# Retention and mixture-of-experts layer: down projections of three groups as three rounded products, centred first pairs, new orders

## The reference

```python
x = x + attn(layernorm(x))
x = x + ffn(layernorm(x))

# attn: 4 heads, q and k of 32, v of 64; q, k get rotary embeddings
scores = einsum('bhtd,bhsd->bhts', q, k) * decay_mask      # gamma_h ** (t - s) for t >= s, else 0
o = einsum('bhts,bhsd->bhtd', scores, v)
o_n = o * rsqrt(mean(o * o, -1) + EPS) * g_norm_w
attn = (o_n * silu(x @ Wg.T)) @ Wo.T

# ffn: 8 experts of which each token takes 2, and a shared expert; all 128 -> 128 -> 128
comb = softmax(x @ gate_w.T), top 2 kept and scaled to sum 1, the others 0
y = sum_e comb[:, e] * (silu(x @ up_w[e] + up_b[e]) @ down_w[e] + down_b[e])
ffn = y + silu(x @ sh_up_w + sh_up_b) @ sh_down_w + sh_down_b
```

## Time and profile before

| | |
|---|---|
| Median of 3 runs (lowest, highest) | 142.51 us (142.03, 142.53) |
| The profiled execution | 142.45 us, of which the span is 140.7 us |
| Busy: PE, PEld, DVE, ACT, POOL | 93%, 74%, 74%, 56%, 35% of the span |
| Mean granted TensorE clock | 0.988 of 2.4 GHz |
| Moved by DMA | 12.50 MB |

### The profile page before, as it was taken

The page is one execution under the profiler, slowest core; times in us unless marked ns, Lnnn a source line. Parts: engine busy times, 40 slices in busy tenths (PEclk is TensorE's granted clock), DMA queues, the critical chain, the costliest instruction groups (busy, mean ns, idle before and its releaser), DMA issues.

```text
span 140.7 us, 3363 instructions
## 1 busy us (share of the span) xinstructions
PE 130.8 (93%) x1249; PEld 103.7 (74%) x1249; DVE 104.2 (74%) x311; ACT 78.6 (56%) x138; POOL 48.8 (35%) x69
## 2 busy tenths in 40 slices
PE   5659899899999999999998999999999999999990
PEld 5549799798978988886885675776557655589990
DVE  3589999989689997998796949679443982113983
ACT  4223937955562478555659762697745864471130
POOL 5458897937372342815222804502000000000000
PEclk9977999999999999999999999999999999999999
DMA  4999910000000000097000097010197200002002
GB/s 113 296 274 317 334 68 0 5 0 5 0 5 0 2 5 0 17 320 270 2 5 0 16 317 270 2 56 19 47 276 283 75 2 0 0 0 79 0 0 75
DMA packets 8659, 12.50 MB, mean 89 GB/s; under 512 B 1298, under 2 KB 5676, under 8 KB 8644
## 3 DMA queue, kind: packets, MB, share of 16 engines
q1 hardware_dynamic: 8356, 12.10, 26.7%
q10 hardware_dynamic: 288, 0.20, 0.4%
HBM read 11.20 MB, written 1.10 MB: 87 GB/s over the span
## 4 chain that ended last, share of the span: by engine, by line
PE 72%; DVE 10%; DMA 5%; SPq 4%; ACT 3%; issue 3%; DVEq 0%
PE bY L1238 17%; PE bU L1061 8%; PE bU L1062 7%; PE bU L1063 7%; DMA UW<-upw 5%; PE bA L1135 5%; PE bA L1211 4%; PE bU L1154 3%; PE bA L1129 3%; PE bA L1105 2%; PE bM L1154 2%; PE bU L1145 2%; PE bM L1180 1%; DVE SC L724 1%; SPq L267 1%
## 5 line engine op out<-in xcount | busy, mean ns | idle before, releaser
L497 ACT ACTIVATE HB<-bU,UB 128x512 f32<-128x512 f32 x36 | 24.3, 686 | 22.0 <-PE bU L1063 21.7
L1238 PE MATMUL bY<-HG,DW 128*128 128x512 f32 x48 | 24.5, 594 | 0.0
L848 DVE TENSOR_TENSOR HG<-CB,HB 128x512 f32<-128x512 f32 x24 | 16.3, 688 | 10.9 <-ACT HB L497 10.2
L353 POOL TENSOR_TENSOR RR<-SS,NHALF 128x8 f32<-128x8 f32 x8 | 13.5, 1684 | 25.9 <-DVE SS L743 25.9
L1061 PE MATMUL bU<-XH,UWH 128*128 128x512 f32 x36 | 21.5, 597 | 0.0
L1062 PE MATMUL bU<-XL,UWH 128*128 128x512 f32 x36 | 14.2, 395 | 0.0
L1063 PE MATMUL bU<-XH,UWL 128*128 128x512 f32 x36 | 14.2, 393 | 0.0
L1061 PEld LDWEIGHTS bU<-XH,UWH 128*128 128x128 f32 x36 | 6.8, 189 | 5.5 <-issue 4.3
L1238 PEld LDWEIGHTS bY<-HG,DW 128*128 128x128 f32 x48 | 8.4, 190 | 2.5 <-issue 1.4
L724 DVE TENSOR_TENSOR SC<-bA,MASK 128x512 f32<-128x512 f32 x16 | 10.2, 679 | 0.0
L1062 PEld LDWEIGHTS bU<-XL,UWH 128*128 128x128 f32 x36 | 6.8, 190 | 3.4 <-issue 3.4
(11 more groups left out here) (180 smaller groups left out, 317.8 us busy)
## 6 DMA issues: line engine op xcount, KB each, us to landing
CB<-scratch SPq DMA_DIRECT2D x12, 512.0 KB, 5.8
ROT<-rotary_tables SPq DMA_DIRECT2D x8, 256.0 KB, 4.5
out<-OUT SPq DMA_DIRECT2D x8, 128.0 KB, 1.8
X<-x SPq DMA_DIRECT2D x7, 128.0 KB, 6.1
UW<-upw SPq DMA_DIRECT2D x1, 576.0 KB, 6.6
DW<-dnw SPq DMA_DIRECT2D x1, 576.0 KB, 5.5
W<-wqkvg SPq DMA_DIRECT2D x1, 256.0 KB, 3.7
W<-wqkvg ACTq DMA_DIRECT2D x1, 128.0 KB, 3.9
```

The lines of the kernel that those rows point to most:

```text
L353: pool.tensor_tensor(RR[:, n], SS[:, n], NHALF[:, 0:2 * H], ALU.pow).then_inc(rr.sem, 1)
L497: act.activation(HB[:, k, :], bU[(g * (E + 1) + k) % 2][:, :], ACT.Silu, bias=UB[:, e:e + 1]).then_inc(hid.sem, 1)
L848: dve.tensor_tensor(HG[:, k % RING, :], CB[:, k - 1, :], HB[:, k, :], ALU.mult).then_inc(gated.sem, 1)
L1238: pe.matmul(bY[:, :], DW[:, e * P:(e + 1) * P], HB[:, 0, :] if k == 0 else HG[:, k % RING, :], start=(k == 0), stop=(k == E)).then_inc(dow ...
```

## The change

Five things are done at once.

1. `down_proj` of groups 0 to 2 becomes a `product` of three matmuls. The weights DW are split once (`split_down` on ScalarE, `low_down` on GpSimd). The gated hidden values are split for each expert: `hi(g, k)` on ScalarE copies to HGH with rounding, `lo(g, k)` subtracts, on VectorE for k = 1, 4, 7 and on GpSimd for the others. HGH and HGL have RING = 3 buffers each. HG itself has 2, so `gating(g, k)` waits for the remainder of k - 2.
2. The first two pairs are centred only (`center1` in place of `normalize1`), so their normalization doesn't wait for the standard deviation. The factor RS1 is applied after the projections: as `scale` of ScalarE's `values` and `gates`, and in `rotary` and `rotate`. Pairs (1, 0) and (1, 1) are normalized on ScalarE, no longer on VectorE.
3. The rotations of pairs (0, 0) to (1, 1) and `low_w(1)` move from GpSimd to VectorE.
4. W's larger part is loaded from ScalarE's queue, behind its smaller part. On SyncE's queue CN falls behind X(3).
5. The orders of all engines and PLACE are laid out anew. XN1 and XN2 hold one group only, SLOTS goes from 4 to 3, TABLES from 6 to 5; the normalizations wait for the transposes of the group before.

```diff
-RING = 4
-SLOTS = 4
-TABLES = 6
-NORM1, NORM2 = 4, 4
+RING = 3
+SLOTS = 3
+TABLES = 5
+LO_V = (1, 4, 7)
+LO_P = (0, 2, 3, 5, 6, 8)
+NORM1, NORM2 = 2, 4
+FOLD = 2
...
+        DWH = sb("DWH", [P, (E + 1) * P], F32R)
+        DWL = sb("DWL", [P, (E + 1) * P], F32R)
...
-        HG = sb("HG", [P, RING, GC])
+        HG = sb("HG", [P, 2, GC])
+        HGH = sb("HGH", [P, RING, GC], F32R)
+        HGL = sb("HGL", [P, RING, GC], F32R)
...
+        def exact(k):
+            return HB[:, 0, :] if k == 0 else HG[:, k % 2, :]
+        def wait_low(eng, g, k):
+            if k in LO_V:
+                eng.wait_ge(g_lo_v.sem, g_lo_v.at(g, LO_V.index(k)))
+            else:
+                eng.wait_ge(g_lo_p.sem, g_lo_p.at(g, LO_P.index(k)))
...
             load_first_x(sp, 0)
-            sp.dma_start(W[:, QK:], wqkvg[:, QK:]).then_inc(ld_w[1].sem, 16)
             load_x(sp, 1)
...
+            def lo(g, k):
+                pool.wait_ge(g_hi.sem, g_hi.at(g, k))
+                pool.tensor_tensor(HGL[:, k % RING, :], exact(k), HGH[:, k % RING, :].bitcast(F32), ALU.subtract).then_inc(g_lo_p.sem, 1)
+            def low_down():
+                pool.wait_ge(dw_hi.sem, 1)
+                pool.tensor_tensor(DWL[:, :], DW[:, :], DWH[:, :].bitcast(F32), ALU.subtract).then_inc(dw_lo.sem, 1)
...
             act.dma_start(W[:, 0:QK], wqkvg[:, 0:QK]).then_inc(ld_w[0].sem, 16)
+            act.dma_start(W[:, QK:], wqkvg[:, QK:]).then_inc(ld_w[1].sem, 16)
...
+            def split_down():
+                act.wait_ge(ld_dn.sem, 16)
+                act.copy(DWH[:, :], DW[:, :]).then_inc(dw_hi.sem, 1)
+            def hi(g, k):
+                if k == 0:
+                    act.wait_ge(hid.sem, hid.at(g, 0))
+                else:
+                    act.wait_ge(gated.sem, gated.at(g, k - 1))
+                if k >= RING:
+                    act.wait_ge(down.sem, down.at(g, k - RING))
+                elif g:
+                    act.wait_ge(down.sem, down.at(g - 1, k + E + 1 - RING))
+                act.copy(HGH[:, k % RING, :], exact(k)).then_inc(g_hi.sem, 1)
...
+            def center1(g, p):
+                dve.wait_ge(mv1.sem, mv1.at(g, p))
+                for b in range(2):
+                    t = g * TILES + 2 * p + b
+                    last = dve.tensor_scalar(XN1[:, p, b * P:(b + 1) * P], X[:, t * P:(t + 1) * P],
+                                             MV1[:, t, 0:1], None, ALU.subtract)
+                last.then_inc(xn1.sem, 1)
...
+                if pair(g, p) < FOLD:
+                    dve.wait_ge(rs1.sem, rs1.at(g, p))
+                    for b in range(2):
+                        t = 2 * pair(g, p) + b
+                        dve.scalar_tensor_tensor(out=RA[:, p, b], in0=src[:, b * QK:(b + 1) * QK], scalar=RS1[:, t:t + 1], in1=cos,
+                                                 op0=ALU.mult, op1=ALU.mult)
...
-                if k > RING:
-                    dve.wait_ge(down.sem, down.at(g, k - RING))
+                if k > 2:
+                    wait_low(dve, g, k - 2)
                 elif g:
-                    dve.wait_ge(down.sem, down.at(g - 1, k + E - RING))
-                dve.tensor_tensor(HG[:, k % RING, :], CB[:, k - 1, :], HB[:, k, :], ALU.mult).then_inc(gated.sem, 1)
+                    wait_low(dve, g - 1, k + E - 2)
+                dve.tensor_tensor(HG[:, k % 2, :], CB[:, k - 1, :], HB[:, k, :], ALU.mult).then_inc(gated.sem, 1)
...
-                pe.matmul(bY[:, :], DW[:, e * P:(e + 1) * P], HB[:, 0, :] if k == 0 else HG[:, k % RING, :], start=(k == 0),
-                          stop=(k == E)).then_inc(down.sem, 1)
+                w = slice(e * P, (e + 1) * P)
+                product(bY[:, :], (DWH[:, w], DWL[:, w]), (HGH[:, k % RING, :], HGL[:, k % RING, :]), k == 0,
+                        k == E).then_inc(down.sem, 1)
...
-            keep_busy(10)
+            keep_busy(7)
             x1_t(0, 0)
+            keep_busy(2)
             x1_t(0, 1)
+            after(xl1, 0, 0)
             proj_qk(0, 0)
             proj_g(0, 0)
             after(xl1, 0, 1)
+            proj_g(0, 1)
             proj_qk(0, 1)
```

More of the change, by code:

```diff
@@ L393, in _ @@
             rstd1(0, 1)
-            low_w(1)
             rstd1(1, 0)
@@ new lines, in _ @@
+            hidden(1, 7)
+            hi(1, 5)
+            hidden(1, 8)
+            hi(1, 6)
+            hidden(2, 0)
+            hi(1, 7)
+            hidden(2, 1)
+            hi(1, 8)
+            hi(2, 0)
+            transposed_out(3, 1)
+            hi(2, 1)
+            hidden(2, 2)
+            sums(1)
+            hi(2, 2)
+            x2_norm(3, 0)
+            hidden(2, 3)
+            hidden(2, 4)
+            x2_hi(3, 0)
+            hi(2, 3)
+            x2_norm(3, 1)
+            hidden(2, 5)
@@ L715, in rotate @@
                 dve.wait_ge(rparts.sem, rparts.at(g, p))
+                if pair(g, p) < FOLD:
+                    for b in range(2):
+                        t = 2 * pair(g, p) + b
+                        last = dve.scalar_tensor_tensor(out=QKR[:, slot(g, p), b], in0=RB[:, p, b], scalar=RS1[:, t:t + 1],
+                                                        in1=RA[:, p, b], op0=ALU.mult, op1=ALU.add)
+                    last.then_inc(rot.sem, 1)
+                    return
                 dve.tensor_tensor(QKR[:, slot(g, p)].rearrange("r b n -> r (b n)"), RA[:, p].rearrange("r b n -> r (b n)"),
@@ new lines, in _ @@
+            proj_qk(2, 1)
+            after(rparts, 2, 0)
+            proj_v(2, 0)
+            proj_out(0, 0)
+            attend(1, 0)
+            after(x1, 0, 0)
+            out_t(0, 1)
+            after(rparts, 2, 1)
+            qk_t(2, 0)
+            after(v_sb, 2, 0)
+            qk_t(2, 1)
+            after(ogt, 0, 1)
+            proj_v(2, 1)
+            after(ogr, 1, 0)
+            scores(1, 1)
+            after(qkt, 2, 1)
+            proj_out(0, 1)
+            after(v_sb, 2, 1)
@@ L1401, in _ @@
-            proj_out(2, 0)
+            up_proj(0, 5)
+            after(xl2, 1, 1)
+            router(1)
+            up_proj(0, 6)
+            after(hid, 0, 5)
+            proj_out(2, 0)
+            after(ogr, 2, 1)
+            proj_g(3, 1)
+            after(x1, 2, 0)
+            out_t(2, 1)
+            down_proj(0, 1)
+            after(hid, 0, 6)
+            qk_t(3, 0)
+            after(ogr, 2, 1)
+            qk_t(3, 1)
             down_proj(0, 2)
+            after(ogt, 2, 1)
+            up_proj(0, 7)
@@ new lines, in _ @@
+            comb_t(2)
+            down_proj(1, 2)
+            after(ogt, 3, 0)
+            up_proj(1, 7)
+            down_proj(1, 3)
+            up_proj(1, 8)
+            down_proj(1, 4)
+            up_proj(2, 0)
+            down_proj(1, 5)
+            up_proj(2, 1)
+            after(hid, 2, 0)
+            proj_out(3, 0)
+            down_proj(1, 6)
+            after(hid, 2, 1)
+            out_t(3, 1)
+            down_proj(1, 7)
+            after(x1, 3, 0)
+            up_proj(2, 2)
```

737 lines of the change are left out of this document (378 added, 359 removed), and 25 rows, old and new, of the table PLACE.

## The result

The changed kernel takes 147.07 us, median of 4 runs (145.21 to 148.63), against 142.27 (141.86 to 142.53) for the kernel before: a ratio of 1.030, 95% interval 1.020 to 1.040. The profiled execution took 147.0 us with a span of 145.3. A time is the median of all runs, while a ratio leaves out runs more than 1.5% above the fastest of the same kernel, so the two can differ a little. I forecast 137.6 with a range of 134.0 to 144.0 and gave slower a chance of 0.17; it is slower, and outside the range.

What follows compares the result with a forecast made beforehand. TensorE was taken to bound the kernel, alone from 91.8 to 124.57 us and level with VectorE earlier. The sum: 142.45 - 4.6 (products) - 2.2 (start) + 2.0 (new waits) = 137.6 us, range 134.0 to 144.0.

Steps and rivals of the forecast that it cites:

- The bound: TensorE alone sets the pace from 91.8 to 124.57 us; before that, from 9.35, TensorE and VectorE run neck and neck.
- The start: Before the first projection: it moves from 9.36 to about 7.1 us, saving 2.2 us.
- the 1.2 us that I had left out of the sum: From 9.35 to 49.9 us: 1.2 us lost at half clock, which shorter gaps at the start may avoid.
- called even: After the start: rotations and normalizations moved to VectorE and ScalarE cost nothing net, bounds -1.5 and +2.
- TensorE's saving: Down projection of three groups: each of 27 products takes 0.69 instead of 0.86 us, 4.6 us saved.
- about 29.7: The stretch from the first to the third group's sums shrinks from 32.77 us to about 29.7.
- the sum's last term: All new waits of TensorE together cost 2.0 us, under half a microsecond at each of four places; bounds 0 and 10.
- I cost it at nothing: low_down on GpSimd in the first 25 us: its 2.65 us are covered by other TensorE work, else cost 2.65.
- half of the collisions, 8 us, fit: From 49.9 to 124.57 us: half of eighteen VectorE-GpSimd collisions, 8 us, fit in VectorE's 12.6 us free; all do not.
- The slower one: Rival: HG's two buffers and the port shared by VectorE and GpSimd make the kernel slower, 144 us; chance 0.25.
- a turn passes 3.7 us: Slower rival's threshold: one turn of HG's two buffers, two experts, forecast at 2.8 or 2.2 us, 4.6 if held.
- The ScalarE rival: ScalarE bounds from 91.8 to 124.57 us, the products' gain is lost and only the start's remains: 140.2 us; chance 0.18.

Runs made afterwards that it cites:

- version 1: The changed kernel with only the products taken back: down_proj plain float32, no hi, lo or low_down, HG four buffers; 139.44 us, ratio 0.977.
- lo_small_down9: The changed kernel with GpSimd's 18 remainder subtractions on 8 columns instead of 512 and low_down in nine pieces; 138.21 us, ratio 0.969.
- hilo_small: The changed kernel with low_down in nine pieces, all 27 remainder subtractions and ScalarE's 27 copies on 8 columns; 135.65 us, ratio 0.952.
- down9: The changed kernel with low_down's one subtraction of 1152 columns made as nine of 128; 143.88 us, ratio 1.005.
- hold_only: Against lo_small_down9: each GpSimd remainder signalled after 8 columns, then 504 columns of weights subtracted that only GpSimd's next remainder waits for; 142.76 us, ratio 1.007.
- lo_pieces: The changed kernel with low_down in nine pieces and each of GpSimd's 18 remainders in four pieces of 128 columns; 144.65 us, ratio 1.018.
- chain_only: Against lo_small_down9: a GpSimd power of 128x6 stands in for each of the 18 subtractions, keeping the latency without the streaming; 138.93 us, ratio 0.978.

## Why the prediction was wrong

**The bound** was read rightly: before, TensorE alone sets the pace from 91.8 on.

**The start** came as forecast: the first projection at 7.04 for a forecast 7.1. The clock stayed at full (1.00 to 46 us), the 1.2 us that I had left out of the sum; but it fell in the next stretch, so over the whole span it gave nothing back (0.985, against 0.988 before). Rotations and normalizations moved to VectorE and ScalarE were called even. With the start and the clock they come to 3.2 us less in version 1, where 2.2 + 1.2 were forecast: no loss shows from them.

**TensorE's saving** is real. In the changed kernel the triples start 0.23 us apart, as forecast:

```profile
98.81 0.40 PE L1212 MATMUL bY<-HGH,DWH 128*128 128x512 f32 x1
...
99.51 0.39 PE L1212 MATMUL bU<-XH,UWH 128*128 128x512 f32 x1
```

These two have two more matmuls between them and are 0.70 us apart. Between the first and third groups' sums, version 1 takes 35.7 us (19.0 and 16.7), lo_small_down9 33.4 and hilo_small 32.8: 2.9 us saved of the 18 x 0.17 = 3.1. Over the whole kernel the ratios fall from 0.977 to 0.952, 3.6 us of the 4.6, with the fixed part of all new instructions still in it. That the stretch would shrink to about 29.7 was wrong for another reason: the new orders put more work there, 35.7 us without any product.

**The step that failed** is the sum's last term, "I take 2.0 us for all the new waits together", with bounds 0 and 10. It measured some 11, give or take 1.6: the ratios from the changed kernel down to hilo_small fall from 1.030 to 0.952, 7.7% or 11 us. Without its last term the sum gives 142.45 - 4.6 - 2.2 = 135.65, and hilo_small measured 135.65. To agree that closely is partly luck, since the clock's 1.2 us and the fixed part of the new instructions are in the one and not in the other. Step by step, each by its ratios, with the noise of the difference:

| what is taken away | forecast | measured |
|---|---|---|
| `low_down` in one piece | nothing | 3.5 us (1.6), part of it the clock |
| the width of GpSimd's 18 remainders | most of 2.0 | 5.1 us (1.4) |
| the width of VectorE's 9 | in the 2.0 | 1.1 us (1.3) |
| the width of ScalarE's copies | in the 2.0 | 1.3 us (0.8) |

The first two lines depend on the order: with the width taken away first they are 6.6 us for the width and 2.0 for `low_down`.

For `low_down` I named the cover only for what is queued behind it on GpSimd ("I cost it at nothing"). The hold, which I had priced for gatings a paragraph later, I did not apply to it: the one instruction of 2.7 us is the longest hold in the kernel. It stands in the stretch where VectorE was at 92%.

For the remainders I had the right mechanism and wrote that "half of the collisions, 8 us, fit". Measured by the group, the gatings alone are 24 x (945 - 688) = 6.2 us longer, and all of VectorE's work together is 8.9 us longer in down9 than in lo_small_down9, so about that much did happen. The step from there was wrong: VectorE's free time over the whole stretch doesn't say that a hold is hidden. TensorE needs `result`, the second sublayer's additions and the router's steps at set moments, all of which stand in VectorE's one queue behind whatever is held (`<-DVE X L888` in the changed kernel, `<-DVE OUT L995` in hold_only, neither of which is held itself). The copies are alike: ScalarE's queue wasn't full, 30.15 of 39.23, and yet they cost 1.3 us.

One reading was too wide. I wrote that GpSimd was idle beside the gatings of the kernel before. Two of them ran wholly inside a GpSimd power and kept their time, which the last section takes up. And the upper bound of a hold, 0.97 us, should be 0.94 by the rows named (1.54 - 0.60), without effect.

**The rivals.** The slower one (144 us, 0.25) had the mechanism; it decided "from the point where a turn passes 3.7 us". That part was mis-sized: a third buffer, which loosens that condition, gives only 1.2 us of 5.1, and the latency alone 1.3. Of its sign, long waits of TensorE for HGL, little was seen: 0.9 us is the longest of the changed kernel. The long ones are for OGR (2.3), X (2.0 and 1.5) and OUT (1.1), results that stand in VectorE's queue behind held work. The ScalarE rival (140.2) had it as the bound, and it isn't the main cost: with the holds gone (lo_small_down9) ScalarE is at 30.32 of 33.38 us in that stretch, 91%, and the kernel is 5.1 us faster all the same; narrowing its copies gives 1.3 more. My price for a copy, 0.51 by starts within bounds of 0.48 and 0.60, was 0.62 by duration in the rows. The chance for slower, 0.17, was too low for a mechanism which the trace of before showed twice.

The Trainium skill (GPSIMD Engine Reference, section "8. Key points"), which I had weighed, was borne out by the 945 ns against 688. A second page would have priced it better: SBUF — State Buffer, section "Who interferes with whom". It says that the port pair which VectorE shares with GpSimd is an exclusive lock, that a VectorE instruction with two SBUF inputs contends for it with a GpSimd one that reads SBUF, and that the order of issue decides who waits. By the same section a reduction stays free, and so does an instruction with at most one SBUF input, unless it runs in a 2-port mode, as a cast can; whoever issues first then has the pair for the whole instruction. The traces agree on the order (67.70 and 68.64 above), on PSUM inputs (68.31) and on a reduction (0.69 us at 84.44, inside a GpSimd subtraction). They differ on "the whole instruction": see the last section.

**What stays open.** Why the cost bends between 256 and 512 columns (0.7 us, then 4.4) no run settles. VectorE's busy time bends with it (2.1 us more, then 6.8), so the holds themselves are few or short at 256 columns; why they are is not shown. Nor is what made the clock fall in the changed kernel's middle stretch, and so whether the 1.7 us estimated for it in the profiled execution belong to `low_down`.

## What to carry to other kernels

Work that goes to an idle GpSimd isn't free when it streams two SBUF tensors: look in the trace for VectorE instructions with two SBUF inputs, and for casts, that start behind it, and price each at the GpSimd instruction's remaining length, plus whatever TensorE waits for in VectorE's queue behind it. One long such instruction is one long hold (2.58 us here); cut it into pieces where nobody waits for the last, and not where somebody does, as lo_pieces shows. Average free time of an engine tells whether work fits, not whether a queue delivers in time. When an experiment changes a width, split it: one kernel that keeps the latency, one that keeps the traffic.

## What the runs showed of the hardware

A GpSimd instruction doesn't always hold VectorE for as long as it runs. In chain_only, GpSimd takes powers of 128x6 numbers, which read SBUF too; VectorE instructions with two SBUF inputs inside them keep their time (chain_only's fence first, then the kernel before, where the power is over 128x8 numbers):

```profile
86.29 1.50 POOL L397 TENSOR_TENSOR PW<-TWO,NHALF 128x6 f32<-128x6 f32 x1
...
86.65 0.42 DVE L945 TENSOR_TENSOR BEF<-DIF,CN 128x256 f32<-128x256 f32 x1
...
90.53 1.33 POOL L397 TENSOR_TENSOR PW<-TWO,NHALF 128x6 f32<-128x6 f32 x1 [2.74 <-ACT HGH L580]
...
90.81 0.19 DVE L976 TENSOR_TENSOR CX<-CMB,CX 128x32 f32<-128x32 f32 x1
```

```profile
76.66 1.64 POOL L353 TENSOR_TENSOR RR<-SS,NHALF 128x8 f32<-128x8 f32 x1 [3.09 <-DVE SS L743]
...
76.82 0.68 DVE L848 TENSOR_TENSOR HG<-CB,HB 128x512 f32<-128x512 f32 x1
```

The first two steps took up to 1.38 and 1.20 us beside subtractions of 512 and 504 columns, and a gating 1.43 at 68.64. So the GpSimd instruction's microseconds alone don't hold VectorE. Whether what counts is the columns that stream or the operation, a power and not a subtraction, no run parts.

A conversion with a single SBUF input can be held as well. In the changed kernel:

```profile
95.21 0.18 DVE L967 CAST CX<-CMB 128x32 fp32r<-128x32 f32 x1
95.23 1.29 POOL L394 TENSOR_TENSOR HGL<-HG,HGH 128x512 fp32r<-128x512 f32 x1 [3.74 <-ACT HGH L574]
95.30 1.27 DVE L968 CAST CX<-CMB 128x32 fp32r<-128x32 f32 x1
```

The second of two equal conversions, 0.07 us behind GpSimd's start, took 1.27 us instead of 0.18. The normalizations of the earlier trace rows, held at 7.43, also read a single SBUF tensor besides one or two numbers per partition.

A GpSimd subtraction of 128 columns took 551 ns on average in lo_pieces and one of 512 columns 1448 in the changed kernel, so four pieces cost half as much again as one.
